# Three stages of a hybrid block: joined at their seams, with the layer norm split by sequence

## What is computed

```
# M, E = 256 inner channels, N = 16 states
x = z * rsqrt(mean(z*z) + eps) * norm_w           # z = LN(x)
skip, xe = x @ skip_w.T, x @ in_w.T
xs = silu(causal_conv4(xe) + conv_b)
delta = softplus(xs @ wd1.T @ wd2.T + wd2_b);  Bm, Cm = xs @ wb.T, xs @ wc.T
h_l = exp(delta_l * A) * h_(l-1) + delta_l * x_l * B_l;  y_l = sum_n h_l * C_l    # over 256 tokens
out = z + ((y + xs * W_D) * silu(skip)) @ out_w.T
# F, two layers: qkv with l2norm and rotary, softmax over a window of 64 in 8 heads, then
#   layer norm, w1, a * gelu(g), w2, + b2
# P, 16 heads of 8: weights ((q.k)^2) * exp(G_t - G_s) under a causal mask, normalised, times v
```

## Time and profile before

| what | us |
|---|---|
| median of three runs | 3156.47 |
| profiled execution | 3154.61 |
| its span, first to last instruction | 3152.8 |
| TensorE busy | 2699.7 (86%) |
| VectorE busy | 2472.1 (78%) |
| ScalarE busy | 2254.9 (72%) |
| GpSimd busy | 1352.2 (43%) |
| mean granted TensorE clock | 0.954 |

### The profile page before, as it was taken

One profiled execution on the slowest core, in us unless ns is written; L12 is line 12 of the kernel. 1 busy time (PEld: TensorE's weight loads), 2 busy tenths in 40 slices (PEclk: granted clock), 3 DMA queues, 4 the chain that ended last, 5 costly groups with the idle time before them and its releaser, 6 DMA issues. The chain is left out here.

```text
span 3152.8 us, 55672 instructions
## 1 busy us (share of the span) xinstructions
PE 2699.7 (86%) x18784; PEld 1825.4 (58%) x18784; DVE 2472.1 (78%) x3831; ACT 2254.9 (72%) x5987; POOL 1352.2 (43%) x1073
## 2 busy tenths in 40 slices
PE   4888888579999999999669999995799999999996
PEld 2444444246666666666447777774566666666664
DVE  6999999767777777777468888887677777777773
ACT  4888888357767677677459999994577766777673
POOL 4666666535545455454310000001445544455452
PEclk9999999789999999999879999997899999999997
DMA  3000000000000000000000000000000000000000
GB/s 88 1 1 1 1 1 1 1 1 2 1 1 1 12 12 1 2 1 1 23 1 2 2 1 2 1 2 1 1 1 1 1 1 12 12 1 1 1 1 27
DMA packets 17237, 17.75 MB, mean 6 GB/s; under 512 B 3997, under 2 KB 14942, under 8 KB 16862
## 3 DMA queue, kind: packets, MB, share of 16 engines
q1 hardware_dynamic: 16958, 14.19, 1.5%
HBM read 12.09 MB, written 2.10 MB: 5 GB/s over the span
## 5 line engine op out<-in xcount | busy, mean ns | idle before, releaser
L906 POOL TENSOR_TENSOR f_p<-f_p,f_rs 128x512 f32<-128x512 f32 (+1 forms) x256 | 320.9, 1253 | 735.9 <-DVE f_rs L855 735.9
L751 ACT ACTIVATE f_p<-pair,f_nm 128x128 f32<-128x128 f32 (+1 forms) x1024 | 389.0, 392 | 192.5 <-DVE f_nm L844 191.7
L898 POOL TENSOR_TENSOR f_qb<-f_kn,f_tab 128x512 f32<-128x512 f32 x256 | 444.2, 1756 | 173.5 <-DVE f_kn L824 173.5
L547 POOL TENSOR_TENSOR m_hc<-m_h,m_c 128x512 f32<-128x512 f32 x256 | 328.5, 1304 | 170.9 <-DVE m_h L509 169.7
L509 DVE TENSOR_TENSOR_SCAN m_h<-m_a,pair 128x1024 f32<-128x1024 f32 x128 | 292.1, 2282 | 2.9
L705 PE MATMUL bank<-f_hnT,f_w 128*128 128x256 f32 (+1 forms) x768 | 214.0, 402 | 80.9 <-DVE f_u L881 77.7
L623 PE MATMUL pair<-f_wqkv,f_hT 128*128 128x512 f32 x512 | 256.9, 625 | 9.8 <-DVE f_kn L824 7.9
L814 DVE TENSOR_REDUCE f_ss<-f_sq 128x16 f32<-128x1024 f32 x128 | 155.2, 1212 | 139.5 <-ACT f_sq L722 139.5
L407 PE MATMUL bank<-m_hc,ident 128*128 128x512 f32 x512 | 258.5, 651 | 4.7 <-POOL m_hc L547 4.7
L666 PE MATMUL pair<-ident,f_p 128*128 128x128 f32 x1536 | 245.8, 283 | 16.6 <-POOL f_p L906 6.9
L1160 POOL TENSOR_TENSOR X<-X,p_y 128x256 f32<-128x256 f32 x16 | 11.7, 730 | 567.6 <-DVE p_y L1154 567.6
(11 more groups left out here) (181 smaller groups left out, 6563.5 us busy)
## 6 DMA issues: line engine op xcount, KB each, us to landing
f_wqkv<-in_f_wqkv SPq DMA_DIRECT2D x4, 768.0 KB, 4.0
X<-in_x SPq DMA_DIRECT2D x16, 128.0 KB, 2.6
out_x<-X SPq DMA_DIRECT2D x16, 128.0 KB, 2.0
f_w<-in_f_w SPq DMA_DIRECT2D x4, 341.0 KB, 3.4
f_wo<-in_f_wo SPq DMA_DIRECT2D x4, 256.0 KB, 2.7
sel<-in_sel SPq DMA_DIRECT2D x1, 768.0 KB
f_w<-in_f_w SPq DMA_DIRECT2D x4, 192.0 KB, 3.2
p_wqk<-in_p_wqk SPq DMA_DIRECT2D x1, 512.0 KB
```

What stands on the lines that cost most here:

```text
L547: op = nc.gpsimd.tensor_tensor(m_hc[:, g % 4, n], m_h[:, g % 2, n], m_c[:, g % 2, n].unsqueeze(1).broadcast_to([P, EC, L]), ALU.mult)
L751: op = nc.scalar.activation(f_p[:, t, j, k0:k1], SC[:, j, k0:k1], ACT.Exp, bias=f_nm[:, t, j:j + 1], accum_out=f_sm[:, t, j:j + 1])
L898: op = nc.gpsimd.tensor_tensor(f_qb[:, t, :, o].rearrange("p (x h) d -> p x h d", x=2), f_kn[:, t, :, 32 - 32 * e:64 - 32 * e].rearrange(" ...
L906: op = nc.gpsimd.tensor_tensor(f_p[:, t, :, k0:k1], f_p[:, t, :, k0:k1], f_rs[:, t, :].unsqueeze(2).broadcast_to([P, 4, k1 - k0]), ALU.mult)
```

## The change

Five things are changed together.

1. Normalisation by sequence. `ln_dve` and `ln_pool` are split in steps for one sequence: st (bn_stats), mv (bn_aggr) and z (one tensor_scalar for each 128 tokens that subtracts and multiplies) on VectorE, ve and rs on GpSimd. Each step waits only for its own sequence.
2. The stages are joined. `START`, `MF`, `FP` and `PF` are lists written out for each engine, in which the last windows of a stage, the normalisation steps and the first windows of the next stage are interleaved; `program` puts the regular windows between them. `run_windows` and `run_layers` go.
3. Buffers are placed so that the tiles of the next stage don't lie on those which the stage before still uses (gaps `f_gap`, `p_gap`, p_e, p_a and p_s as separate tiles).
4. Inputs in parts: x comes in five transfers of 1, 1, 2, 4 and 8 sequences, each with its own semaphore; ScalarE issues the 13 weights of M, SyncE the rest; every output sequence is stored after its own last step.
5. In M, xs * W_D is added by TensorE (a product with the diagonal tile m_skip in the group of y7), so VectorE's ys goes; xr goes from VectorE to ScalarE; the window's order and lags are new. In F and P the copy zc goes and the transposes read Z. F's second layer writes to X: GpSimd adds b2 to X early (xb), zb adds X, and the two wide additions X + Z go.

```diff
-    "sq me rr xr xT xe skip u bc ue z",
+    "sq me rr xr xT xe skip u bc ue z r1 delta lo bx0 h0",
-    "dve": "bx5 h5 r1 bx6 delta h6 lo bx7 xr h7 bx0 h0 bx1 ys h1 yg bx2 h2 x bx3 h3 ue bx4 h4",
-    "act": "a0 xTe c0 a1 sq c1 a2 xs c2 a3 c3 a4 gate a5 c4 abs c5 exp hi a6 ln mid2 c6 c7 mid a7",
+    "dve": "bx1 h1 bx2 yg h2 bx3 h3 ue bx4 x h4 bx5 h5 r1 bx6 delta h6 lo bx7 h7 bx0 h0",
+    "pe": "bB7 bB0 y4 bB1 bC0 y5 y6 bC1 y7 bB2 xT bC2 bB3 xe bC3 skip bB4 u bB5 out bc bC4 z bC5 y0 bB6 y1 bC6 y2 y3 "
+        "bC7",
+    "act": "xTe sq c2 a3 xs c3 gate a4 c4 a5 abs c5 exp hi ln a6 mid2 a7 c6 mid a0 c7 a1 c0 xr a2 c1",
+    "pool": "dx hc6 xx hc7 me rr hc0 hc1 hc2 hc3 hc4 hc5"}
...
+MF = {
+    "dve": "n1: st m17: bx1 n2: st m17: h1 n3: st n4: st m17: bx2 yg n1: mv m17: h2 n2: mv n3: mv m17: bx3 n4: mv "
+        "m17: h3 bx4 x h4 n1: z m17: bx5 h5 n5: st m17: bx6 f1: hT m17: h6 bx7 h7 f1: ss0 cl0 n5: mv n2: z f1: kn0 "
+        "qa0 n6: st n7: st n8: st n9: st f1: qs0 ss1 cl1 n10: st f1: kn1 m18: yg f1: qa1 n6: mv n11: st n7: mv n8: "
...
+def program(eng):
+    yield from join(eng, START[eng], {"n": 0})
+    yield from span(eng, "m", START_M + 1, MF_M - 1)
+    yield from join(eng, MF[eng], {"n": NSEQ})
+    yield from span(eng, "f", MF_F + 1, FP_F - 1)
+    yield from join(eng, FP[eng], {"n": 2 * NSEQ})
+    yield from span(eng, "p", FP_P + 1, PF_P - 1)
+    yield from join(eng, PF[eng], {"n": 3 * NSEQ, "f": 2 * NSEQ})
+    yield from span(eng, "f", PF_F + 1, 2 * NSEQ + 2, 2 * NSEQ)
...
             elif k == "y":
-                pe.wait_ge(*pool_m.at(i, f"hc{g}"))
                 if g == 0:
                     pe.wait_ge(*dve_m.at(i - 1, "x"))
+                pe.wait_ge(*pool_m.at(i, f"hc{g}"))
                 for n in range(GN):
                     mm = nc.tensor.matmul(bank[1][:], ident[:], m_hc[:, g % 4, n].rearrange("p c l -> p (c l)"),
-                                          start=g == 0 and n == 0, stop=g == NG - 1 and n == GN - 1)
+                                          start=g == 0 and n == 0, stop=False, skip_group_check=True)
+                if g == NG - 1:
+                    if i == 1:
+                        pe.wait_ge(m_set, 3)
+                    for c in range(EC):
+                        mm = nc.tensor.matmul(m_y_ps[:, c, :], m_skip[:, c, :], m_xs[:, b, c, :], start=False,
+                                              stop=c == EC - 1, skip_group_check=True)
...
+            elif s == "xr":
+                act.wait_ge(*pe_m.at(i - 1, "xT"))
+                act.wait_ge(*pool_m.at(i, "rr"))
+                for t in range(T):
+                    op = nc.scalar.activation(m_xr[:, t, :], tiles(seq(Z, i))[:, t, :], ACT.Copy, scale=m_rr[:, t:t + 1])
...
+            elif s == "mv":
+                dve.wait_ge(ln_st, i)
+                for t in range(T):
+                    op = nc.vector.bn_aggr(lmv[:, q, t, :], lst[:, q, t, :])
+                op.then_inc(ln_mv, 1)
+            elif s == "z":
+                dve.wait_ge(ln_rs, i)
+                for t in range(T):
+                    op = nc.vector.tensor_scalar(z[:, t, :], x[:, t, :], lmv[:, q, t, 0:1], lrs[:, q, t:t + 1],
+                                                 ALU.subtract, ALU.mult)
+                op.then_inc(ln_z, 1)
...
             if s == "xT":
-                pe.wait_ge(*dve_f.at(i, "zc"))
...
                 pe.wait_ge(*act_f.at(i - 1, "Te11"))
-                for t in range(T):
-                    mm = nc.tensor.transpose(bank[0][:, t * P:t * P + P], f_zc[:, t * P:t * P + P], ident[:])
+                if n % 2:
+                    pe.wait_ge(ln_z, n * NSEQ + at)
+                else:
+                    pe.wait_ge(*dve_f.at(i - NSEQ, "z2"))
+                for t in range(T):
+                    mm = nc.tensor.transpose(bank[0][:, t * P:t * P + P], tiles(seq(Z, at))[:, t, :], ident[:])
...
-                op = nc.vector.tensor_tensor(seq(Z, z_at), f_zb[:], bank[1][:, 0:L], ALU.add)
+                op = nc.vector.tensor_tensor(seq(Z if n % 2 else X, at), f_zb[:], bank[1][:, 0:L], ALU.add)
...
+            for t, name in m_first:
+                act.dma_start(t, ins[name]).then_inc(m_first_loaded, 16)
+            for t, name in m_last:
+                act.dma_start(t, ins[name]).then_inc(m_last_loaded, 16)
```

More of the change, by code:

```diff
@@ L80, in done @@
         return self.streams[self.stage[step]].done(step)
-def run_windows(eng, stages, step, count):
-    n = 1 + max(stages.stage.values())
-    def window(k, parity, live):
-        for s in stages.order:
-            lag = stages.stage[s]
-            if lag in live:
-                step(s, k - lag, (parity - lag) % 2)
-    for k in range(1, count + n):
-        window(k, k % 2, [lag for lag in range(n) if 1 <= k - lag <= count])
 F_STAGES = [
[1 row of a table removed]
[1 row of a table added]
     "T00 Te00 T01 Te01 T10 T11 Te10 Te11 p00",
@@ L134 @@
 M_STAGES = [
[5 rows of a table removed]
-M_ORDER = {
-    "dve": "bx5 h5 r1 bx6 delta h6 lo bx7 xr h7 bx0 h0 bx1 ys h1 yg bx2 h2 x bx3 h3 ue bx4 h4",
-    "pe": "bC7 y4 y5 bB0 bC0 xT bB1 bC1 y6 y7 xe bB2 bC2 out skip bB3 bC3 u bC4 bB4 y0 y1 bB5 z bB6 bC5 bc bC6 y2 y3 "
-        "bB7",
-    "act": "a0 xTe c0 a1 sq c1 a2 xs c2 a3 c3 a4 gate a5 c4 abs c5 exp hi a6 ln mid2 c6 c7 mid a7",
-    "pool": "hc0 hc1 hc2 me hc3 rr hc4 hc5 dx hc6 xx hc7"}
-def run_layers(eng, stages, step, count):
-    n = 1 + max(stages.stage.values())
-    assert n == 3 and count % 2 == 0
-    def window(k, parity, live, layer_of):
-        for s in stages.order:
-            lag = stages.stage[s]
-            if lag in live:
-                layer = layer_of(lag)
-                step(s, layer, k - lag - layer * count, (parity - lag) % 2)
-    for k in range(1, 2 * count + n):
-        window(k, k % 2, [lag for lag in range(n) if 1 <= k - lag <= 2 * count], lambda lag: int(k - lag > count))
[4 rows of a table added]
@@ new lines, in span @@
+def span(eng, ph, first, last, base=0):
+    for k in range(first, last + 1):
+        yield from window(eng, ph, k, base)
+def program(eng):
[7 more added lines that the diff above has]
+    yield from span(eng, "f", PF_F + 1, 2 * NSEQ + 2, 2 * NSEQ)
@@ L165, in build, with run @@
+def run(eng, step):
+    for ph, s, i in program(eng):
+        step(ph, s, i)
 def build(nc, ins, out):
@@ L1248, in _, with step @@
+            def step(ph, s, i):
+                if ph == "c":
+                    first(s)
+                elif ph == "n":
+                    ln_dve(dve, s, i)
+                elif ph == "m":
+                    m_dve(dve, s, i, i % 2)
+                elif ph == "f":
+                    f_dve(dve, s, i, i % 2, *layer_of(i))
+                else:
+                    p_dve(dve, s, i, i % 2)
+            run("dve", step)
         @block.gpsimd
```

534 lines of the change are left out of this document (297 added, 237 removed), and 95 rows, old and new, of tables (FP, F_STAGES, MF, M_STAGES).

## The result

The changed kernel took **3022.64 us** (median of four runs, 3021.49 to 3025.83), the kernel before in the same session 3155.26 (3153.13 to 3156.8): a ratio of 0.9583, with a 95% interval of 0.957 to 0.9595, so 4.2% faster. The forecast was 3020 us. The profiled execution of the changed kernel, the slowest of its four, took 3025.83 us with a span of 3024.0, against the 3152.8 of the earlier trace rows; its mean granted TensorE clock is 0.975. One of all the executions behind this document, of the experiment with more table loads, took 7625.78 us for a reason that isn't known, and its ratio leaves it out.

What follows compares the result with a forecast made beforehand. Prediction: VectorE limits M, TensorE F, ScalarE P, and nothing overlaps between stages. Terms sum to −135.8 us from a span of 3152.8, giving 3017.0; with 3.7 on top the forecast is 3020 us, range 2988 to 3058.

Steps and rivals of the forecast that it cites:

- Start, -20 forecast: Start of the kernel: first convolution at about 13 instead of 33.6 us, so −20 us for everything behind.
- M's window, -2.0 forecast: Stage M: xr and ys leave VectorE, net −2.0 us a window, from 34.2 to 32.2; −30 us in all.
- VectorE over 97% busy: Sign for stage M: M's repetition at 32.2 us with VectorE over 97% busy and xr on ScalarE.
- Rival A: Stage M: a wait replaces the removed work, window stays at 34.2, −30 becomes 0, 3050 us; chance 9%.
- Rival D: Stage M: TensorE becomes the bound at its lower clock, +350 us, some 3370 in all; chance 2%.
- bB7 and lo, about 1 us ahead: M's new order: these narrowest places come about 1 us ahead of their use, so VectorE stays the limit.
- rival P: M and F's first windows: every z beside a busy GpSimd costs 1.28 us instead of 0.65, +32, 3052; chance 7%.
- The term of +14: M's second and third window: ten z at 1.3 us and 1 us of mv on full VectorE, +14 us (5 to 26).
- F to P, -58 forecast: Seam F to P: 139.1 us become 81, 70 us of TensorE work plus 15%, −58 us (bounds −69, −30).
- Rival B: Seam F to P gives half, as chains of short steps wait for each other: −35, 3043 us; chance 12%.
- P to F, -11 forecast: Seam P to F: 18.2 us without TensorE go, moved steps cost +2.2 and +5; −11 us (−17 to 0).
- M to F, +8: F's first three windows: 12 us of moved normalisation steps show, warmer TensorE returns about 4; net +8 us (0 to 22).

Runs made afterwards that it cites:

- The last experiment: Changed kernel with own engine's waits first in bx and h, p_qT's clear early, and xs ahead of the exponential of A_log at the start: 3007.98 us.
- The two experiments: Changed kernel with scan h waiting first for its own engine's product: 3017.67 us; the same with product bx also waiting first for its own scan: 3010.74 us.
- the experiment gives zc: Changed kernel with F's copy zc put back on VectorE and TensorE transposing the copy: 3028.88 us.

## Why the prediction was right, and where not

The time lay 2.6 us above the forecast and inside its range, and the seams, undone one by one, were worth about what was expected of them. Three terms had the wrong size and their errors partly cancel (+4.2, +10.2, -5.8 us), and M's window was right by two errors that cancel; so the closeness of the total is in part luck.

**Start, -20 forecast, -15.8 measured.** The convolution came at 14.1 (13 forecast). What came after it was late, ScalarE first (start, duration, operation, idle before):

```profile
8.92 1.28 ACT L555 ACT_TABLE_LOAD   x1 [8.92 <-issue]
...
19.89 0.23 ACT L1392 ACTIVATE m_A<-m_A_log 128x32 f32<-128x32 f32 x1 [5.80 <-DMA sel<-in_sel]
...
22.02 0.84 ACT L577 ACTIVATE m_xs<-pair,m_conv_b 128x256 f32<-128x256 f32 x2
```

The squares are held by the 13 issues, as forecast (10.2 instead of 8.7). The failed step was "33.6 to 13 is -20 us for everything behind": from the first convolution to the first scan it was 17.7 us before and 21.5 now. The sum took the length of this chain from a kernel in which all loads and norms were done when it began. Both traces show what its links added. First, the exponential of A_log waits until 19.89 for sel, 768 KB and the last of M's transfers, with the second sequence's squares and a table load behind it, so xs comes at 22.0, 1.5 us after the convolution's end at 20.5 (39.84 after 39.81 before). Then the two products up to ue take 3.68 us, from 23.00 to 26.68, at a granted clock of 0.55, after 2.5 us in which TensorE had nothing; before they took 2.14 at 1.00. The rest of the chain is 0.5 us longer.

Mending these two alone would not have helped. VectorE's list holds, ahead of ue (m_u), a step that waits for sel until 19.89 and statistics and z of later sequences, so ue could not have come much before 26.74 in any case. The last experiment shows it: xs came at 19.3 and the product for ue had ended at 22.4, at a clock of 1.00, yet VectorE, which ahead of ue also waits for the exponential that the edit had moved 1.6 us back, reached ue only at 28.15 (first the changed kernel, then the experiment's VectorE and TensorE):

```profile
26.74 0.40 DVE L621 COPY m_u<-bank 64x256 f32<-64x256 f32 x1
```
```profile
28.15 0.38 DVE L621 COPY m_u<-bank 64x256 f32<-64x256 f32 x1
...
28.64 2.05 PE L520 MATMUL pair<-m_u,m_wd 65*128 65x256 f32 x4 [5.27 <-DVE m_u L621]
```

Putting ue ahead of the later sequences' steps was not tried.

**M's window, -2.0 forecast, -1.97 measured, by an account that was wrong in two places.** From the two group views, per window: xr 18.3/13 = 1.4 us went (1.47 forecast), two ys 0.87 (0.85), and 0.2 us of idle time ahead of the products came, as allowed. Not forecast were lo, 12.0/13 - 5.8/14 = 0.51 us less (the one window that the prediction had looked at, had it at 0.41), and the idle time ahead of scans, 10.3/14 - 2.3/13 = 0.56 us more. These two cancel, and that is luck. The prediction read the changed list for what stands between products and scans, but not the order of the waits, which is in the change and in the idle time that it had itself divided by 128. The two experiments price it at 0.42 a window for the scan's side (about 5 us of time), and as much for the product's side, which the kernel before had too. For the same reason the sign "VectorE over 97% busy" failed: it was busy 305.48 of 321.68 us, 95% (330.35 of 341.34, 97%, before). Rival A (the window stays at 34.2) fell: in 129 us VectorE waited 0.7 us for the exponentials, and no other wait for another engine shows. Rival D fell too: PE's clock in those ten windows was 0.98, its busy time 284.55 of 321.68. The claim of the new order's slack ("bB7 and lo, about 1 us ahead") was sound, but the loads were counted as ScalarE's time only; the experiment with four loads shows that they can cost VectorE 3.05 us a window.

The z were priced at 0.65 to 0.75 us beside GpSimd and 0.27 without. Here are the z of M's first rounds, and then all of them (count, min/median/max ns, first and last start, shape):

```profile
L704 DVE TENSOR_SCALAR Z<-X,lmv,lrs x20: 314/548/4255, 49.5 to 116.6; 128x128 f32<-128x128 f32 x20
```
```profile
L704 DVE TENSOR_SCALAR Z<-X,lmv,lrs x128: 308/341/4255, 5.3 to 2154.6; 128x128 f32<-128x128 f32 x128
```

A median of 0.55 in M's first rounds, beside a busy GpSimd, and 0.34 over all: rival P, in which each beside a busy GpSimd would cost 1.28, fell. The price without GpSimd was taken too low, 0.27: the least of all z is 0.31. Two z, halves of one sequence, took 4.1 and 4.3 us while GpSimd cleared F's and P's tiles between 83.4 and 87.5 us, five memsets that the prediction did not price. The term of +14 can be read by itself: the first three intervals between like scans are 34.8, 41.2 and 34.8 us, 14.2 more than three of 32.17. By an estimate from the length of these two z, 3 to 4 us of that are the memsets', so the z alone were dearer in the forecast than in fact. With 15.75 windows of -1.97, which are -31.0, that leaves +6.6 of the measured -10.2, where the forecast had +4.5; in it are M's last rounds, and that the kernel before had shorter windows at its ends (33.05 the first, 32.08 the last).

**F to P, -58 forecast, -47.8 measured: the term that was mis-sized most.** The stretch of 139.1 us that the prediction worked from has become 91.3, 30% above its floor of 70 us of TensorE work at full clock. The floor was right in kind: in the 102.8 us of the stage table TensorE was busy 88.25, at 0.93. The allowance of 15% for waits between the lists was too small. Of the missing 10.2 us, about 4 are the cast behind the clear, which the prediction had put in "GpSimd's idle time" at no cost; the others are spread waits, 12.4 us of TensorE idle even in the better seam, and its clock. Rival B (half the gain, -35) lay in the right direction; the measured -47.8 stands between it and the forecast, a little nearer to the forecast.

**P to F, -11 forecast, -16.8 measured (about -15 by the other traces).** Half or more of the charge of 7.2 us for the moved steps fell away: VectorE's idle time in that stretch takes them (28.0 us are still left). The same kind of charge at M to F, +8, was met (+8.5), with a clock of 0.84 in F's first windows (0.81 in the earlier trace rows), so the 4 us that a warmer TensorE was to return came only in part.

**F and the end.** F's usual interval moved by 0.07 us, from 28.07 to 28.00, and the experiment gives zc the whole of it; F's and P's own windows stayed at what the earlier trace rows showed. From the end of the last z2 to the end of the span it is 2.3 us, as against 2.4 worked out:

```profile
3021.35 0.42 DVE L1039 TENSOR_TENSOR X<-f_zb,bank 128x256 f32<-128x256 f32 x1 [3.02 <-PE bank L862]
```

## What to carry to other kernels

When stages are joined, count the idle time around the seam and the fullest engine's work in it at full clock; then walk through each engine's list and ask what stands behind each long instruction, on its own engine and, for VectorE and GpSimd, on the other of the two. An instruction that nobody waits for (a clear, a table load) still may have a place where it is free and others where it costs its full length or more (here 3.5 us for a cast, 3.05 us a window for two loads and the new place of xs). On an engine that is some 95% busy read the idle time per pair of instructions, and when an edit reorders waits, count that as a change of its own. When a total comes out right, add up its terms one by one before trusting them: here a window was right to 0.03 us by two errors of 0.5. And look which windows a mean is made of; the first and last of a pipelined stage are not like the others.

## What was not expected of the hardware

- **Order of waits.** Of several waits ahead of a VectorE instruction, the one for VectorE's own last result costs 0.13 us of idle time when it comes last, and 0.03 when it comes first (both experiments on M's waits). By what mechanism is not shown.
- **A clear on GpSimd stops VectorE's cast.** 0.70 us became 4.15 beside a memset that only writes SBUF; with the clear moved away it was 0.70 again, in three different kernels, and 0.28 where GpSimd did nothing large. The Trainium skill (SBUF — State Buffer, Who interferes with whom) says that a cast or tensor_scalar can enter a mode that needs the port pair shared with GpSimd and then waits for the other's whole instruction; the trace agrees, 4.15 us ending with the clear.
- **Two operands in SBUF.** A VectorE product of two SBUF tiles that starts while GpSimd's product is running waits for it: lo took 1.07 to 1.42 us in the 8 of 16 windows of the kernel before in which a GpSimd product was under way, ending 0.28 us after it, and 0.41 in the others, also in those where GpSimd began 0.05 us later. yg took 1.06 us behind such a product and 0.67 ahead of one. The same section of the Trainium skill says that a VectorE instruction with two SBUF inputs contends with a GpSimd instruction that reads SBUF, and that one with a single SBUF input, outside the modes above, does not. The trace agrees (with one operand in PSUM yg took 0.68 us beside the end of a GpSimd product), but no run here moved GpSimd's products alone.
